# Rope attentions: prefetch in pieces, clears moved, fills of the stacked operands as two DMAs of nine part products

## The reference, cut to what matters

```
h = layernorm(x) * (1 + ca) + sa
x = x + ga * attention(h)
h = layernorm(x) * (1 + cb) + sb
x = x + gb * ffn(h)
```

```
q, k, v = split(h @ Wqkv)            # (16 heads, 256, 8) each
Q = q * cos + rotate(q) * sin        # the same for K
scores = Q @ K^T / sqrt(8)           # causal
y = softmax(scores) @ v
out = y @ Wproj
```

## Time and profile before

| | us |
|---|---|
| median of three executions | 3025.16 |
| the profiled execution, its time | 3025.41 |
| the profiled execution, its span | 3023.7 |
| TensorE matmul busy | 2683.4 (89%) |
| VectorE busy | 2218.1 (73%) |
| ScalarE busy | 1444.7 (48%) |
| GpSimd busy | 579.4 (19%) |
| first rope stage, about | 1926 to 2256 |
| second rope stage, about | 2494 to 2815 |

### The profile page before, as it was taken

The page is one execution under the profiler, slowest core; times in us unless marked ns, Lnnn a source line. Parts: engine busy times, 40 slices in busy tenths (PEclk is TensorE's granted clock), DMA queues, the critical chain, the costliest instruction groups (busy, mean ns, idle before and its releaser), DMA issues. The chain is left out here.

```text
span 3023.7 us, 67058 instructions
## 1 busy us (share of the span) xinstructions
PE 2683.4 (89%) x21108; PEld 2309.7 (76%) x21108; DVE 2218.1 (73%) x6616; ACT 1444.7 (48%) x4145; POOL 579.4 (19%) x1032
## 2 busy tenths in 40 slices
PE   6999999998999899999998999579976765999786
PEld 5988888897888799999997999456654543666565
DVE  4888888886776477777776777457759985777797
ACT  3666666665555466666663223135542221545321
POOL 0000000000111000000000111167751214776111
PEclk9999999999999999999998999789995556999899
DMA  5000000002000544444441000222220002222000
GB/s 137 2 2 1 1 1 1 1 1 59 1 0 4 157 151 146 147 147 146 146 151 31 1 0 0 88 73 75 72 59 8 0 0 78 75 72 68 1 0 28
DMA packets 137064, 160.83 MB, mean 53 GB/s; under 512 B 9360, under 2 KB 127520, under 8 KB 135832
## 3 DMA queue, kind: packets, MB, share of 16 engines
q1 hardware_dynamic: 136856, 158.43, 17.8%
HBM read 92.32 MB, written 64.96 MB: 52 GB/s over the span
## 5 line engine op out<-in xcount | busy, mean ns | idle before, releaser
L134 POOL TENSOR_TENSOR hT<-hT 128x256 fp32r<-128x256 f32 x64 | 46.8, 731 | 1470.5 <-ACT hT L127 1470.5
L118 PE MATMUL bank<-hT,a_xA 128*128 128x256 f32 x768 | 228.3, 297 | 5.7 <-ACT a_p L429 3.0
L572 DVE TENSOR_REDUCE a_nmax<-bank 128x2 f32<-128x512 f32 x256 | 174.9, 690 | 58.3 <-PE bank L120 56.2
L119 PE MATMUL bank<-hT,a_xA 128*128 128x256 f32 x768 | 217.4, 283 | 0.0
L120 PE MATMUL bank<-hT,a_xA 128*128 128x256 f32 x768 | 216.9, 282 | 0.0
L1647 ACT ACTIVATE a_p<-bank 128x1024 f32<-128x1024 f32 (+1 forms) x256 | 193.4, 808 | 23.3 <-PE bank L1703 19.2
L1021 ACT ACTIVATE a_p<-a_p,a_nmax 128x256 f32<-128x256 f32 x256 | 128.1, 501 | 135.1 <-DVE a_nmax L1205 135.1
L450 ACT CAST a_xA<-bank 128x256 fp32r<-128x256 f32 x256 | 94.8, 372 | 200.8 <-PE bank L120 200.8
L1286 ACT ACTIVATE f_silu<-bank 128x512 f32<-128x512 f32 x128 | 76.5, 597 | 214.6 <-PE bank L120 214.5
L814 PE MATMUL bank<-arena,f_hidden 128*128 128x128 f32 x1024 | 171.6, 288 | 6.3 <-DVE f_acc L868 5.0
L751 ACT ACTIVATE f_hidden<-bank,arena 128x256 f32<-128x256 f32 x256 | 120.3, 472 | 114.4 <-PE bank L120 113.1
(11 more groups left out here) (287 smaller groups left out, 8584.3 us busy)
## 6 DMA issues: line engine op xcount, KB each, us to landing
pos_dram<-a_pos SPq DMA_DIRECT2D x128, 383.0 KB
a_shifted<-pos_dram SPq DMA_DIRECT2D x128, 256.0 KB, 2.7
cut_dram<-a_cut SPq DMA_DIRECT2D x64, 192.0 KB, 3.8
a_stack<-cut_dram SPq DMA_DIRECT2D x128, 96.0 KB
gate<-gates_dram SPq DMA_DIRECT2D x8, 1024.0 KB, 17.2
a_stack<-cut_dram SPq DMA_DIRECT2D x128, 64.0 KB
arena<-in_task SPq DMA_DIRECT2D x1, 4624.0 KB, 14.3
a_stack<-cut_dram SPq DMA_DIRECT2D x128, 32.0 KB
```

Of the source, the lines that this page charges most:

```text
L118: pe.matmul(out, left[0], right[0], start=start, stop=False, skip_group_check=True)
L119: pe.matmul(out, left[0], right[1], start=False, stop=False, skip_group_check=True)
L572: dve.tensor_reduce(nmax[:, at.ring(2), h, :], s_ps[h][:].rearrange("p (t k) -> p t k", t=NT), AX_X, ALU.max, negate=True).then_inc(s["nma ...
```

## The change

Three things change in the rope stages, and one in all phases.

1. **Prefetch in pieces.** In a rope stage the prefetch is no longer issued at the start. It is cut into pieces (`task` into four, every other tensor whole, the gate into four) and step s = 0, 1, 2, ... of the first items issues one piece each, after the step's other DMAs. For ffn2 that are nine pieces of weights and four of the gate, for ffn3 four and four. In the other phases, the prefetch stays where it is, but the gate comes in four DMAs.
2. **Clears.** GpSimd clears the whole stack in two operations. VectorE clears v behind the rotation terms of the first item's q. TensorE waits for the rows of ones only before the first scores.
3. **Fills.** The stack takes all nine part products, 72 rows. q is written with its parts as before, into a DRAM tensor that also holds a row of zeros (written once at the start, waited for); k in three DMAs, each as soon as its part is cut. A fill is two DMAs: 75 rows for q (each of 25 DRAM rows three times in a row; the last three are the zeros), 72 rows for k (24 DRAM rows, the whole three times over). The contraction on TensorE spans 128 partitions before and after.

```diff
--- before.py
+++ after.py
@@ -20,6 +20,10 @@
 LN_EPS = 1e-5
 MASKED = -1e30
 ARENA = 6912, 10624
+
+
+GATE_PIECES = 4
+PIECES = {"task": 4}
 
 
 class Step:
@@ -296,15 +300,41 @@
 
 def load_gate(sp, k, phase):
 
-    sp.dma_start(k.gate[phase % 2][:], k.gates_dram[:, phase, :].partition_broadcast(P)).then_inc(k.gate_in[phase], 16)
+    for g in range(GATE_PIECES):
+        load_gate_piece(sp, k, phase, g)
+
+
+def load_gate_piece(sp, k, phase, g):
+
+    n = NB // GATE_PIECES
+    sp.dma_start(k.gate[phase % 2][:, g * n:(g + 1) * n], k.gates_dram[g * n:(g + 1) * n, phase, :].partition_broadcast(P)
+                 ).then_inc(k.gate_in[phase], 16)
 
 
 def load_weights(sp, nc, k, d, phase):
+
+    for piece in range(weight_pieces(phase)):
+        load_weight_piece(sp, k, d, phase, piece)
+
+
+def weight_pieces(phase):
+
+    return sum(PIECES.get(name, 1) for name, _, _ in WEIGHTS[phase])
+
+
+def load_weight_piece(sp, k, d, phase, piece):
 
     at = 0
     for name, shape, parts in WEIGHTS[phase]:
-        size = int(np.prod(shape))
-        sp.dma_start(k.arena[phase % 2][0:parts, at:at + size], d[name]).then_inc(k.weights_in[phase], 16)
+        size, cuts = int(np.prod(shape)), PIECES.get(name, 1)
+        if 0 <= piece < cuts:
+            part = size // cuts
+            whole = d[name]
+            if cuts > 1:
+                whole = whole[:, piece * part:(piece + 1) * part]
+            sp.dma_start(k.arena[phase % 2][0:parts, at + piece * part:at + (piece + 1) * part], whole
+                         ).then_inc(k.weights_in[phase], 16)
+        piece -= cuts
         at += size
     assert at <= ARENA[phase % 2]
 
...
@@ -1430,10 +1460,11 @@
 def rope_attention(nc, d, k, phase):
 
     PER, H, DH, PARTS, G = 4, 16, 8, 3, 4
-    ROWS = DH * sum(PARTS - a for a in range(PARTS))
+    ROWS = DH * PARTS * PARTS
     SHIFTS = 2
+    QROWS = DH * PARTS + 1
     VP = 144 * G
-    FILLS = 2 * PARTS + 1
+    FILLS = 2
     n = k.norms
     w = weights(k, phase)
     for name in list(w):
...
@@ -1459,12 +1490,13 @@
         shiftT = sb("shiftT", [SHIFTS * 2 * G, 2, T], BF16)
         rec = sb("rec", [P, NT, H])
         spare = sb("spare", [P, 2])
-        cut_dram = nc.dram_tensor(f"cut_dram{phase}", (2, PARTS, 2, DH * H, T), BF16, kind="Internal").ap()
+        cut_q = nc.dram_tensor(f"cut_q{phase}", (2, QROWS, H, T), BF16, kind="Internal").ap()
+        cut_k = nc.dram_tensor(f"cut_k{phase}", (2, DH, PARTS, H, T), BF16, kind="Internal").ap()
         s_ps, sT_ps, o_ps, misc_ps = k.psum[:, 0:6 * T], k.psum[:, 6 * T:12 * T], k.banks[6], k.banks[7]
         names = ("chain", "var", "std", "rstd", "xn", "ht_mm", "ht", "q_mm", "q_terms", "k_mm", "k_terms", "cut",
                  "written_q", "written_k", "v_mm", "v", "s_mm", "nmax", "shift_hi", "shift", "shiftT_mm", "shiftT",
                  "sT_mm", "exp", "causal", "spare", "o_mm", "o", "back_mm", "rec", "on", "oT_mm", "oT", "y_mm", "res", "blank", "v0", "ones_set",
-                 "ones_in")
+                 "ones_in", "zeros_in")
         s = signals(nc, ctx, f"a{phase}_", names + tuple(f"{x}{a}{b}" for x in ("stacked", "shifted")
                                                          for a in range(2) for b in range(2)))
         written = [s["written_q"], s["written_k"]]
@@ -1497,8 +1529,13 @@
 
             @block.sync
             def _(sp):
-                prefetch(sp, nc, k, d, phase)
-                ROW = H * DH * T
+
+                def prefetch_piece(s):
+
+                    if 0 <= s < weight_pieces(phase + 1):
+                        load_weight_piece(sp, k, d, phase + 1, s)
+                    if 0 <= s - weight_pieces(phase + 1) < GATE_PIECES:
+                        load_gate_piece(sp, k, phase + 1, s - weight_pieces(phase + 1))
 
                 def constant_rows(rows, count):
 
@@ -1508,19 +1545,16 @@
                 def fill(at, half):
 
                     wait(sp, written[0], at, 16, item=True)
-                    wait(sp, written[1], at, 16, item=True)
+                    wait(sp, written[1], at, 16 * PARTS, item=True)
                     sem, heads = stacked[place(at)][half], slice(8 * half, 8 * half + 8)
-                    for which in range(2):
-                        row = 0
-                        for a in range(PARTS):
-                            rows = (PARTS - a) * DH
-                            start = (place(at) * PARTS * 2 + (1 if which else 2 * a)) * ROW + 8 * half * T
-                            src = bass.AP(cut_dram.tensor, start,
-                                          [[2 * ROW if which else 0, PARTS - a], [H * T, DH], [1, 8 * T]])
-                            sp.dma_start(stack[row:row + rows, place(at), which, heads].rearrange("r h t -> r (h t)"),
-                                         src).then_inc(sem, 16)
-                            row += rows
-                    sp.dma_start(stack[ROWS:ROWS + SHIFTS, place(at), 0, heads], constant_rows(zeros, 8)).then_inc(sem, 16)
+                    q_rows = bass.AP(cut_q.tensor, place(at) * QROWS * H * T + 8 * half * T,
+                                     [[H * T, QROWS], [0, PARTS], [1, 8 * T]])
+                    k_rows = bass.AP(cut_k.tensor, place(at) * (QROWS - 1) * H * T + 8 * half * T,
+                                     [[0, PARTS], [H * T, QROWS - 1], [1, 8 * T]])
+                    sp.dma_start(stack[0:ROWS + PARTS, place(at), 0, heads].rearrange("r h t -> r (h t)"), q_rows
+                                 ).then_inc(sem, 16)
+                    sp.dma_start(stack[0:ROWS, place(at), 1, heads].rearrange("r h t -> r (h t)"), k_rows
+                                 ).then_inc(sem, 16)
 
                 def shift_rows(at, half):
                     wait(sp, s["shiftT"], at, 2, 1 - half, item=True)
@@ -1528,14 +1562,24 @@
                                  ).then_inc(shifted[place(at)][half], 16)
 
                 def write(at, which):
-                    wait(sp, s["cut"], at, 10, 5 - 5 * which, item=True)
-                    sp.dma_start(cut_dram[place(at), :, which].rearrange("a r t -> r a t"), cut[:, :, which]
-                                 ).then_inc(written[which], 16)
-
+                    if which:
+                        for a, done in enumerate((6, 9, 10)):
+                            wait(sp, s["cut"], at, 10, 10 - done, item=True)
+                            k_rows = bass.AP(cut_k.tensor, (place(at) * (QROWS - 1) + a) * H * T,
+                                             [[PARTS * H * T, DH], [T, H], [1, T]])
+                            sp.dma_start(k_rows, cut[:, a, 1]).then_inc(written[1], 16)
+                    else:
+                        wait(sp, s["cut"], at, 10, 5, item=True)
+                        sp.dma_start(cut_q[place(at), 0:QROWS - 1].rearrange("(a r) h t -> (r h) a t", a=PARTS), cut[:, :, 0]
+                                     ).then_inc(written[0], 16)
+
+                sp.wait_ge(s["ones_set"], 1)
                 sp.wait_ge(s["blank"], 2)
-                sp.wait_ge(s["ones_set"], 1)
                 for x in range(2):
                     sp.dma_start(stack[ROWS:ROWS + SHIFTS, x, 1], constant_rows(ones, H)).then_inc(s["ones_in"], 16)
+                for x in range(2):
+                    sp.dma_start(cut_q[x, QROWS - 1:QROWS], constant_rows(zeros, H)).then_inc(s["zeros_in"], 16)
+                sp.wait_ge(s["zeros_in"], 32)
 
                 def step(at):
                     ni, pi = at.shift(PER), at.shift(-PER)
@@ -1555,12 +1599,15 @@
                             fill(ni, 0)
                         if at.real:
                             shift_rows(at, 0)
+                    if isinstance(at.base, int) and at.base == 0:
+                        prefetch_piece(at.s)
 
                 walk(sp, PER, 4, LEAD, LAG, step)
 
             @block.gpsimd
             def _(pool):
-                pool.memset(stack[:, 1].rearrange("p a h t -> p (a h t)").bitcast(F32), 0.0).then_inc(s["blank"], 1)
+                for x in range(2):
+                    pool.memset(stack[:, x].rearrange("p a h t -> p (a h t)").bitcast(F32), 0.0).then_inc(s["blank"], 1)
                 pool.memset(spare[:], 0.0).then_inc(s["spare"], 1)
                 pool.wait_ge(s["spare"], 1)
 
@@ -1572,7 +1619,7 @@
                             pool.wait_ge(s["cut"], at.item * 10 + 5 * which + m)
 
                     wait(pool, terms_ready, at, item=True)
-                    wait(pool, written[which], at.shift(-PER), 16, item=True)
+                    wait(pool, written[which], at.shift(-PER), 16 * PARTS if which else 16, item=True)
                     x, y, c = terms[:, which, 0, :], terms[:, which, 1, :], cut[:, :, which, :]
                     link(pool.tensor_tensor(c[:, 0], x, y, ALU.add), 1)
                     link(pool.tensor_tensor(rotated[:, which], x, y, ALU.add), 2)
...
@@ -1651,8 +1699,7 @@
 
             @block.tensor
             def _(pe):
```

(28 more changed lines are left out.)

49 lines of the change are left out of this document (25 added, 24 removed).

## The result

| | median | lowest to highest | runs |
|---|---|---|---|
| before | 3025.72 us | 3025.08 to 3027.16 | 4 |
| changed | 3075.91 us | 3074.43 to 3078.73 | 4 |

The ratio is 1.0166, with a 95% interval of 1.0149 to 1.0184. The forecast was 3054, its range 3010 to 3085: slower was right, and so was the mechanism, but the size was 22 us short, and 3076 lies just outside the likeliest case's own range, 3035 to 3072.

A forecast was written before the change was run, and what follows sets the result against it. Rope-stage starts were bound by waiting for the ones behind the gate, items by TensorE and the DRAM path, both 16.8 us. Starts +0.5 - 1.8, items -25.3, clock -2: 28.6 slower, 3054 us, range 3010 to 3085.

The forecast's parts named there:

- likeliest case: The prediction's main case for the whole kernel: slower, at 3054 us, own range 3035 to 3072, chance 0.48.
- the clock: After new waits of several us, TensorE runs at 1.2 GHz for a while: 2 us lost.
- Starts: Rope stages' first transposes come earlier without the wait for the ones: 25.3 us in the first stage, 13.9 in the second.
- covered: At the stage's start, GpSimd's two clears (2 x 3.5 us) end by 1932.9, before its first parts at 1934.8, costing nothing.
- Clears of v: Clears between the first item's q and k rotations on VectorE delay the first k parts by 1.7 us.
- S: Time one fill takes on the first, most loaded DMA engine: 5.8 us before, forecast 6.8 after, ends 4.8 and 7.8.
- The sentence on issuing: Six fewer DMAs per fill save some 3 us on SP's queue, but gain nothing because the engines finish later.
- The loop of an item: Fills, writes and landing in series on the first engine take 17.9 us per item against 16.8: 1.1 more each.
- 2S + 4.3: First engine's time per item: two fills of S, plus 4.3 us for shift DMAs, q and k writes, landing and start.
- The prefetch in pieces: Pieces among the first items' fills, 2.6 to 2.8 us per task piece, give back all but 0.5 of 22.6 us.
- The gate's price: A gate piece among the first items' fills costs between 0.9 and 3.7 us; 2 was taken.
- Wide fills: Rival: the merged fill DMAs spread over more engines, making the kernel faster, priced at 2990 us; chance 0.17.

The follow-up runs named there:

- e10: Changed kernel with fills on 12 engines, weights prefetched in front, gate pieces spread, v cleared before the first q rotation, GpSimd's stack clears after the first normalised rows: 2968.5 us.
- e1: Changed kernel with each fill as five DMAs, q and k both spread over 12 engines, same rows and nearly the same bytes: 2987.4 us.
- e2: As e1, five DMAs with the same rows and bytes, but those of q and k with outermost count 3, on 3 engines each: 3154.3 us.
- e3: Changed kernel with only the q side of the fill respread over 12 engines, zero rows in their own DMA, k still on 3: 3034.9 us.
- e12: Changed kernel with only the prefetch's weights moved to the stage's start, the gate still in pieces between fills: 3059.5 us.
- e4: Changed kernel with the prefetch issued whole at the stage's start, gate still in four DMAs; new fills, writes and clears of v kept: 3055.8 us.
- e8: Kernel before with its old fills, writes and products, plus the later wait for the ones and moved clears; prefetch whole in front, gate in four DMAs: 3002.1 us.
- e7: Kernel before with its old fills, writes and products, plus only the start half of the change: moved clears, later wait for ones, prefetch in pieces: 3022.4 us.

## Why the prediction was right in kind and short in size

Between the profiled spans the sum was 22.8 us short (51.4 against 28.6). No single term carries that: the steady items 8.5, the first transposes 5.1, from there to the first scores 4.3, the first items behind them 4.1, the ends of the stages 5.2, less the 2 put down for the clock and the 2.5 by which the first rope stage began earlier.

1. **Starts, 2.5 us short in each stage.** The first transposes were forecast at 1930.7 and came at 1930.71; that is luck, for the stage began 2.5 us earlier in this profile. Counted from TensorE's last work before the stage they came after 10.91 us instead of 33.70, 22.8 earlier where 25.3 was forecast, and in the second stage after 10.69 instead of 21.94, 11.3 earlier where 13.9 was forecast. The step that failed is "covered" for GpSimd's two clears: they hold VectorE up (last section). With them out of the way, e10 has 6.47 and 6.25.
2. **Clears of v, short.** They were priced at 1.7 us. TensorE waits 4.52 us for the k rotation behind them and 0.79 for the q rotation without them; before it waited 0.78 for each. First scores came 27.6 us after the first transposes where the forecast had 24.9: 1958.27 against 1955.6.
3. **The fill, right.** S was forecast at 6.8 with engines counted by outermost dimension; the halves of item 0 are 6.53 and 6.79 apart. The shares of 0.31 in the q part and 0.19 in the k part, and e1 against e2, show the count. The Trainium skill ("DMA: Bandwidth & Descriptors", "Why a DMA increments its semaphore by 16 and not by 1") gives five and three engines for these shapes, and the trace agrees. The sentence on issuing counts six fewer DMAs per fill; seven became two, five fewer.
4. **The loop of an item, right in kind.** 17.9 us forecast, 18.10 and 18.40 measured. The law 2S + 4.3 holds no better than that: at S = 8.64 it gives 21.6, and e2 showed 20.6 to 20.9. That TensorE's 16.8 still hides an S of 5.8 is shown by e3's later items. Over 23 items this term came to 33.8 instead of 25.3, the largest single miss.
5. **The prefetch in pieces: priced too low.** "A task piece is 1156 KB at 456 GB/s, 2.6 to 2.8 us": that rate is of transfers alone on the engines. Beside fills, and queued between them, the trace shows 315 and 260 GB/s; 1156 KB at 260 is 4.4 us. Items 0 to 3 stood 21.4, 28.6 and 20.9 apart where the forecast had 19.7, 26.5 and 17.8. (Its own terms for item 1 add up to 1975.0, not 1975.3; two later steps are off by 0.1 and 0.2.) The working has some 10 us for the weights' pieces of the first stage (1.2, 0.5, 5.6 and 2.8); e12 puts them at 16.3 there (104.1 against 120.4), and at 11 to 16 us in the whole kernel. The gate's price, on which the working dwelt, was not the trouble (e12 against e4: 4 to 5).
6. **The comparison that was missing.** The forecast compared pieces with the prefetch as it stood before, and took the 25.8 us of the gate for the price of standing in front. e4 and e8 show that most of that was the wait for the ones, not the transfers: with the prefetch in front, e4's first scores come 6.0 us later than in the changed kernel, but 13.9 earlier than before. Dropping that wait, with the clears moved, is worth 18 us (e8), and cutting up the prefetch takes them back (e7).
7. **Left out.** 2.0 us behind item 15's first scores in the first stage, and 3.2 in the second. That it is the last item's own steps, as slow as elsewhere, is likely but was not measured. The 2 us for the clock can't be told apart from the waits.
8. **The rivals.** "Wide fills" (2990) was not what this change does, but it is what e1 does: 2987.

What stays open: why between the changed kernel and e2 an item grows by only 1.0 (first stage) to 1.2 us (second) for each us of S, and not by 2, and what share of the 33.8 us of steady loss the three k writes have. The edit that would settle the second, one k write on 16 engines, wasn't tried.

## What to carry to other kernels

Count a DMA's engines from its outermost dimensions before merging transfers: fewer, larger DMAs can be served by fewer engines, and 167 us lay between two kernels with the same bytes, rows and number of DMAs (e1 and e2). Where a transfer is waited for too long, ask first whether it must be waited for there at all; move the wait before you cut up or move the transfer. And price a transfer by the rate that it has in its new place, beside what runs there, not by the rate that it had alone.
